# Group matmuls in four row tiles, a conditional residual layer on one Trainium2 core

## What is computed

```
masked_w = weight * mask[None, :, :]                 # (g, o, t)
w_bot    = einsum('bg,got->bot', y, masked_w)        # one 512 x 512 matrix for each batch
out      = x + einsum('bnt,bot->bno', x, w_bot) + bias
```

## Time and profile before

| | |
|---|---|
| median of 3 runs | 603.37 us |
| profiled execution, its own time | 604.59 us |
| its span, first to last instruction | 602.80 us |
| mean granted TensorE clock | 0.997 |
| TensorE matmuls, busy | 592.4 us (98%), 6343 records |
| VectorE busy | 320.9 us (53%) |
| ScalarE busy | 142.3 us (24%) |
| data moved | 148.33 MB, mean 246 GB/s |

### The profile page before, as it was taken

How to read it: one execution, slowest core, us unless ns; L and a number is a source line. 1 busy time by engine, 2 the same in 40 slices (tenths; PEclk the granted TensorE clock), 3 DMA queues, 4 the chain that set the end, 5 groups by cost and what they waited for, 6 DMA issues and landing times.

```text
span 602.8 us, 14826 instructions
## 1 busy us (share of the span) xinstructions
PE 592.4 (98%) x6343; PEld 515.1 (85%) x6343; DVE 320.9 (53%) x525; ACT 142.3 (24%) x278; POOL 36.3 (6%) x33
## 2 busy tenths in 40 slices
PE   7899999999999999999999999999999999999998
PEld 5799988888888888888888888888888888888886
DVE  4565445546546556465565565555554654654342
ACT  5343222222222222222222222222222222220000
POOL 3330000000000113231000000000000000000000
PEclk8999999999999999999999999999999999999999
DMA  8976557676776899998766776767767776778852
GB/s 324 406 280 197 199 176 228 235 236 223 230 247 207 295 333 336 352 318 284 247 214 227 251 212 240 233 228 227 241 229 228 237 235 229 225 232 258 296 160 87
DMA packets 60833, 148.33 MB, mean 246 GB/s; under 512 B 6736, under 2 KB 9552, under 8 KB 60768
## 3 DMA queue, kind: packets, MB, share of 16 engines
q1 hardware_dynamic: 40176, 113.00, 58.2%
q10 hardware_dynamic: 20592, 34.39, 15.1%
HBM read 113.81 MB, written 33.55 MB: 244 GB/s over the span
## 4 chain that ended last, share of the span: by engine, by line
PE 94%; DMA 4%; issue 1%; DVE 1%; SPq 0%; POOL 0%; DVEq 0%; POOLq 0%
PE ps L446 73%; PE ps L423 20%; DMA staged<-in_xn 3%; DMA xs<-in_mask 1%; PE ps L406 0%; DVE staged L356 0%; POOL wm L193 0%; SPq L214 0%; DVE wbot L328 0%; DVE wm L193 0%; SPq L229 0%; SPq L220 0%; DVE staged L361 0%; DVE staged L342 0%; DVEq L165 0%
## 5 line engine op out<-in xcount | busy, mean ns | idle before, releaser
L446 PE MATMUL ps<-wbot,xs 128*128 128x256 f32 (+1 forms) x2176 | 459.3, 370 | 1.8 <-DVE wbot L328 1.5
L446 PEld LDWEIGHTS ps<-wbot,xs 128*128 128x128 f32 x2176 | 389.7, 190 | 56.6 <-issue 3.6
L328 DVE COPY wbot<-ps 128x512 f32<-128x512 f32 (+2 forms) x271 | 163.8, 650 | 208.7 <-PE ps L446 181.0
L268 ACT ACTIVATE wbot<-ps 128x512 f32<-128x512 f32 (+2 forms) x277 | 141.1, 568 | 399.4 <-PE ps L423 198.0
L423 PEld LDWEIGHTS ps<-y_sb,wm 32*128 32x128 f32 x4096 | 124.1, 188 | 23.4 <-issue 21.1
L423 PE MATMUL ps<-y_sb,wm 32*128 32x128 f32 x4096 | 137.2, 279 | 3.8 <-DVE wm L193 1.6
L356 DVE TENSOR_TENSOR staged<-ps,staged 128x512 f32<-128x512 f32 x111 | 76.2, 687 | 39.3 <-PE ps L446 39.1
L342 DVE TENSOR_TENSOR staged<-staged,bias_sb 128x512 f32<-128x512 f32 x112 | 78.4, 700 | 11.6 <-DMA staged<-in_xn 11.3
L193 POOL TENSOR_TENSOR wm<-wm,mask_sb 128x512 f32<-128x512 f32 x16 | 20.4, 1298 | 215.5 <-DMA mask_sb<-in_mask 215.5
L356 DVE TENSOR_TENSOR staged<-ps,bias_sb 128x256 f32<-128x256 f32 (+1 forms) x24 | 12.2, 510 | 12.9 <-PE ps L446 10.8
L193 POOL TENSOR_TENSOR wm<-wm,xs 128x512 f32<-128x512 f32 x12 | 15.1, 1270 | 23.0 <-DMA xs<-in_mask 22.9
(11 more groups left out here) (2 smaller groups left out, 0.2 us busy)
## 6 DMA issues: line engine op xcount, KB each, us to landing
xs<-in_x SPq DMA_DIRECT2D x128, 512.0 KB, 3.9
out<-staged ACTq DMA_DIRECT2D x119, 256.0 KB, 4.8
staged<-in_xn SPq DMA_DIRECT2D x112, 256.0 KB, 4.3
wm<-in_w SPq DMA_DIRECT2D x12, 512.0 KB, 7.0
mask_sb<-in_mask SPq DMA_DIRECT2D x8, 512.0 KB, 6.5
out<-staged ACTq DMA_DIRECT2D x18, 128.0 KB, 4.0
wm<-in_w SPq DMA_DIRECT2D x8, 256.0 KB, 5.6
xs<-in_mask SPq DMA_DIRECT2D x4, 512.0 KB, 12.8
```

The costliest lines, as they stand in the source:

```text
L268: eng.activation(tile_place(b, j, first, end), tile_sums(b, j, first, end), ACT.Copy).then_inc(s_ev_a, 1)
L328: eng.tensor_copy(tile_place(b, j, first, end), tile_sums(b, j, first, end)).then_inc(s_ev_v, 1)
L446: ins = eng.matmul(bank[:, at_h:at_h + width], xs[:, n % XRING, h, k, :], at, start=(k == 0), stop=(k == KT - 1))
```

## The change

TensorE works on pairs of pieces, four batches. Each of the four batches has a PSUM bank of its own. A pair is made in four **turns**: in turn t, batch i uses row tile (i + t) mod 4, that is 32 of the 128 rows of its contraction, over the four chunks of t; after four turns each batch has been through all row tiles, and its bank holds the whole sum. From the second turn on, batch i waits for the semaphore `s_turn[i]`, which its own last matmul of the former turn raises. The array stays in four row tiles for bursts and groups alike.

Bursts stand between the turns: in a usual pair half of the first burst after turn 0, its other half after turn 1, the second burst after turn 2 (`bursts_in`). Pairs and bursts use four banks each and swap them from pair to pair (`bank_of`, `USED`, `FORMER`): the bursts of a pair use the four banks of the pair before, one burst after the other in the same four, and the next pair takes them after that. The pair that opens a unit (`halved`, units 1 to 7) is made for its first 128 columns in four turns, with bursts after turns 1 and 2, and then for its other 128 in four more without bursts. Pairs 0 to 7 are the pieces of 128 columns; pair 4 has no burst. From piece 122 on, when all bursts are done, pieces are made as before on the whole array (`plain`); the last is made and stored in three parts (256, 128 and 128 columns).

VectorE's order in a pair: both additions of the pair before, the copies of the first burst, x+bias for the two pieces of the pair, the copies of the other bursts. A piece's sums are free to add once its whole pair is done (`done_at`). ScalarE: two stores, then the copies. SyncE loads x in twos; x for the addition goes ahead of them, and x step 7 ahead of the last w pair. SOON is 2, the mask of burst 7 goes to GpSimd, and tile 1 of burst 3 to VectorE.

```diff
+ENDING = ((0, 0, SL), (1, 0, SL // 2), (1, SL // 2, SL))
+PAIRS = (LAST + 1) // 2
+def bursts_in(p):
+    if p < EARLY // 2:
+        return {0: ((2, 8, 0, KT),),
+                1: ((0, 9, 0, 2), (1, 9, 2, KT), (2, 10, 0, KT)),
+                2: ((0, 11, 0, KT), (1, 12, 0, KT), (2, 13, 0, KT)),
+                3: ((0, 14, 0, KT), (2, 15, 0, KT))}[p]
+    b = 2 * p + 2 * CS - 26
+    if p == EARLY // 2 or b >= BURSTS:
+        return ()
+    if halved(p):
+        return ((1, b, 0, KT), (2, b + 1, 0, KT))
+    return ((0, b, 0, 2), (1, b, 2, KT), (2, b + 1, 0, KT))
+def halved(p):
+    u, g, _, _ = PIECES[2 * p]
+    return u > 0 and g == 0
+def done_at(m):
+    return TILES * (m // 2 + 1) if m < PLAIN else TILES * PLAIN // 2 + m - PLAIN + 1
...
+USED = [[], []]
+for _b in range(HALF):
+    USED[_b % 2].append(("burst", _b))
+for _p in range(PLAIN // 2):
+    USED[_p % 2].append(("pair", _p))
+    USED[1 - _p % 2] += [("burst", _b) for _b in bursts_of(_p)]
...
-BY_VECTOR = (0, 1, 3, 7)
+BY_VECTOR = (0, 1, 3)
...
+            for n in range(XRING, STEPS, 2):
+                m = DONE_WITH[divmod(n - XRING, GROUPS)]
+                if m + 4 >= OWN_X:
+                    load_xn(m + 4)
+                    load_xn(m + 5)
                 load_x(n)
+                load_x(n + 1)
+                if m // 2 in LOAD_W_AT:
+                    load_w(1, LOAD_W_AT[m // 2], 2)
...
+            for p in range(PLAIN // 2 + 1):
+                if p:
+                    add_sums(2 * p - 2)
+                    add_sums(2 * p - 1)
+                bursts = bursts_of(p)
+                for b in bursts[:1]:
                     evict(b)
+                for m in (2 * p, 2 * p + 1):
+                    if m >= OWN_X:
+                        add_bias_to_x(m)
+                for b in bursts[1:]:
+                    evict(b)
...
+            def turn(p, t, c, end, opening, closing, last):
+                u, g, first, _ = PIECES[2 * p]
+                cols = slice((c - first) * CO, (end - first) * CO)
+                for k in range(KT):
+                    for i in range(TILES):
+                        j = (i + t) % TILES
+                        rows = slice(j * TR, (j + 1) * TR)
+                        gi, h = g + i // GB, i % GB
+                        if opening and k == 0 and c == first:
+                            room(("pair", p), i)
+                        if not opening and k == 0:
+                            eng.wait_ge(s_turn[i], turns[0])
+                        at = sums[rows, gi, c:end, k, h, :] if u % 2 else sums[rows, c:end, gi, k, h, :]
+                        ins = eng.matmul(ps[:, p % 2 * TILES + i, cols], xs[rows, (u * GROUPS + gi) % XRING, h, k, :], at,
+                                         start=opening and k == 0, stop=closing and k == KT - 1)
+                        if k == KT - 1:
+                            ins.then_inc(s_s2 if last else s_turn[i], 1)
+                turns[0] += 0 if last else 1
+            def pair(p):
+                u, g, c, end = PIECES[2 * p]
+                first_end = HALF if halved(p) else end
+                group_ready(u, g, first_end)
+                group_ready(u, g + 1, first_end)
+                for t in range(TILES):
+                    turn(p, t, c, first_end, t == 0, t == TILES - 1, t == TILES - 1 and not halved(p))
+                    for at, b, step, to in IN_PAIR[p]:
+                        if at == t:
+                            burst(b, step, to)
+                if halved(p):
+                    group_ready(u, g, end)
+                    for i in range(TILES):
+                        turn(p, i + TILES - 1, first_end, end, i == 0, i == TILES - 1, i == TILES - 1)
```

More of the change, by code:

```diff
@@ L377, in _, with room, burst @@
         def _(eng):
[L378 to L389, removed]
+            def room(key, j):
+                former = FORMER[key]
+                if former is None:
+                    return
+                kind, at = former
+                if kind == "pair":
+                    eng.wait_ge(s_o, 2 * at + 2)
+                else:
+                    tile_evicted(eng, at, j, GROUPS)
+            def burst(b, step, end):
                 u, c = divmod(b, CS)
@@ L409, in add_x @@
                             ins.then_inc(s_s1, 1)
[L411 to L419, removed]
+                if step == 0:
+                    if b == 0:
+                        eng.wait_ge(s_y, 16)
+                    if b == CS:
+                        eng.wait_ge(s_y_rest, 16)
+                    if win == 0:
+                        masked(eng, s, c)
+                    if ahead:
+                        add_x()
@@ L420, in burst @@
+                for k in chunks[step:end]:
                     for j in range(TILES):
-                        if not ahead and k == others[0]:
-                            room((b, j))
-                        ins = eng.matmul(bank[j][:, k * P:(k + 1) * P], wm[rows[j], c, k * P:(k + 1) * P],
+                        if not ahead and k == chunks[0]:
+                            room(("burst", b), j)
+                        ins = eng.matmul(at(j, k), wm[rows[j], c, k * P:(k + 1) * P],
                                          y_sb[rows[j], win, :], start=not (ahead and k == own),
@@ L425, in burst, with group_ready @@
                                          stop=not (behind and k == own))
-                        if not behind and k == (others[-1] if ahead else own):
+                        if not behind and k == chunks[-1]:
                             ins.then_inc(s_s1, 1)
-                if behind:
+                if end == KT and behind:
                     add_x()
-            def piece(m):
-                u, g, c, end = PIECES[m]
+            def group_ready(u, g, end):
                 n = u * GROUPS + g
-                width = (end - c) * CO
@@ L435, in piece @@
                 eng.wait_ge(s_x[n % XRING], 16 * (n // XRING + 1))
                 if g in (0, SOON):
+                    b = u * CS + end - 1
+                    soon = g == 0 and len(parts_of(b)) > TILES
                     for j in range(TILES):
[L438 to L443, removed]
+                        tile_evicted(eng, b, j, SOON if soon else GROUPS)
@@ L452, in _ @@
             for _ in range(WARM):
-                eng.matmul(ps[BANKS - 1][:, :], zeros[:, 0:P], zeros[:, 0:BANK], start=True, stop=True)
+                eng.matmul(ps[:, BANKS - 1, :], zeros[:, 0:P], zeros[:, 0:BANK], start=True, stop=True)
             for b in range(HALF):
[L455 to L459, removed]
+                burst(b, 0, KT)
+            for p in range(PLAIN // 2):
+                pair(p)
+            for m in range(PLAIN, LAST + 1):
+                plain(m)
 LEAD = {_c: _c if _c < HALF else _c - _c % 2 for _c in range(CS)}
```

135 lines of the change are left out of this document (71 added, 64 removed).

## The result

The changed kernel took **635.7 us** (median of 4 runs, 630.7 to 650.5) against 603.2 before: 1.051 times as long, 95% interval 1.043 to 1.060. The forecast was 603.2, with a range up to 612. Slower was given 0.40, but not by so much.

What follows compares the result with a forecast made beforehand. TensorE, busy 98%, bounds the kernel. New work of 531.7 us against 531.2 gives +0.5; with -0.3 for mask 7 and -0.4 at the end, -0.2 us: median 603.2 us, no change, range 597 to 612.

Steps and rivals of the forecast that it cites:

- The round trip between the forms: Switching TensorE between bursts and groups costs 0.42 us; 61 such trips, 25.6 us, removed but half of the last.
- The wide slot in row tiles: 256-column slots in row tiles, taken as 0.216 us; rival: 2.7 ns more each, +4.0 us, 607.2; chance 0.12.
- Two copies in the shadow of a wide turn: Between a pair's bursts in the same banks: 1.78 us wait covered by a wide turn's 1.84, 0.06 to spare.
- A turn behind another: Turn directly after another waits for the same batch's former turn: 0.31 us lost, 34 uncovered turns, 10.5 us.
- An opening pair: Halved pair opening units 1 to 7: about 11.0 us against 9.2, its four uncovered turns included.
- Instructions: Rival: doubled TensorE instruction stream; one in five of 100 packets costing 1.25 us, +25, 628; chance 0.05.
- the cover of the additions: First burst of a wide pair waits for the former pair's additions: 1.93 us against 1.94, so nothing lost.
- To VectorE 0.11: Latency from a pair's last matmul record to VectorE's additions, 0.11 us within the 1.93 us wait.
- covers are too short: Rival: three waits in each of 46 wide pairs not covered; at 0.08 us longer latency +9.4, 612.6; chance 0.19.
- late VectorE: In the kernel before, 2.3 us lost between 209 and 253 us, VectorE late behind its loads; taken as removed.

Runs made afterwards that it cites:

- e6: Changed kernel's order, banks and loads, but each batch made on the whole array where its turn stood; 652.2 us, 1.080 of the kernel before.
- e2: Changed kernel without the loads of x transposed beyond the first ten steps, 62 MB less moved; 620.4 us, 1.027 of the kernel before.
- e1: Changed kernel run once more with no edit, for its trace and spread of times; 641.6 us, 1.059 of the kernel before.
- e12: Kernel before with its steady x and x+bias loads of two groups asked for together; 602.9 us, 0.9975 of the kernel before.
- e5: Changed kernel with the second x and x+bias load of each two held until the next pair's second turn is done; 622.9 us, 1.030 of the kernel before.
- the first trace: First profiled execution of the changed kernel, the longest of its four runs; 650.5 us.
- e4: Changed kernel with one semaphore increment and one wait a turn in place of four; 642.5 us, 1.060 of the kernel before.
- e7: Changed kernel with one increment in place of four at a pair's end only, turns keeping four; 643.6 us, 1.056 of the kernel before.
- e9: Kernel before with sixteen already satisfied waits (eight instructions) after each group matmul; 1137 us.

## Why the prediction was wrong

**What held.** The round trip between the forms costs 0.41 to 0.42 us and goes away (e6). The wide slot in row tiles is 0.216 us, so that rival is out. Two copies in the shadow of a wide turn fit. A turn behind another cost less than the 0.31 I took: its first matmul starts 0.33 us after the last slot began, where 0.11 is the pace, so 0.22, and its four waits come 0.04 us apart. An opening pair undisturbed takes 11.14 us for 11.05 (e2), which is partly luck: its four turns were 0.36 us cheaper than taken, so the rest was some 0.45 dearer.

**The step that failed** is the rival "Instructions", which the sum put at nothing. It was named, tied to the 1.25 us of "issue" in the earlier trace rows, priced at 25 us (one in five of 100 packets), and given 0.05, with the ground that "bursts issue at twice the new mean rate without a pause". A burst is 32 weight loads and 32 matmuls, 64 instructions in 0.9 us, after which groups issue 9 a microsecond; a short rush is no measure of what can be sustained. The mean went from 21 records a microsecond (12,894 of TensorE in 603 us) to 41 (26,367 in 637), and the instruction packets from 50 to 103:

```profile
q8 instruction: 103, 1.69, 1.1%
```

Stops came at 19 and 20 of the 103 blocks of 256, up to 3.3 us long, 17.6 to 25.5 us a run. The packets in the traces show what they are. In all 14 traces there is one packet of q8 (16 KB) for 256 records of TensorE: 103 for 26,367, 86 for 22,143, 60 for 15,342, 50 for 12,894. Of 1158 such blocks not one began less than 1.2 us after the end of its packet, and the 111 stops of over 0.31 us at the start of a block all ended 1.2 to 1.6 us after it; the one that ended at 278.22 us in e1 had its packet from 276.0 to 276.9. A packet lasts 0.95 to 0.98 us in the median of every run, so its own transfer is not what grows. What differs is when it starts, here counted from TensorE's entry into the block ahead of the one it brings (60 to 545 us of each trace):

| us | packet starts after: median, 90% within, longest | a block lasts: median, shortest |
|---|---|---|
| kernel before | 0.5, 3.6, 4.3 | 11.1, 6.6 |
| its loads in twos (e12) | 1.1, 4.5, 5.6 | 11.1, 6.6 |
| whole array (e6) | 0.8, 3.2, 4.8 | 12.7, 9.0 |
| changed kernel (e1) | 1.8, 3.9, 4.6 | 5.9, 4.2 |
| without x loads (e2) | 0.4, 1.3, 4.2 | 5.7, 4.2 |
| loads spread (e5) | 0.9, 2.8, 4.6 | 5.7, 4.2 |

The kernel before gets packets 4 us late too, and a block of 6.6 us or more hides it. In a block of 5.9 us, a packet that starts over some 3.7 us late (5.9 less 0.96 and 1.2, an estimate) stops TensorE. So it is the instructions per microsecond that failed. e6 alone would not show it, since it also lacks the turns' waits and has three round trips a pair. That data transfers have a part in how late a packet starts is shown by e2 and e5, and e12 has later packets than the kernel before without a stop. Why a packet starts late in one block and not in the next stays open.

**A second, smaller step**: what a stop does to the clock. The prediction counted no clock at all. 6.8 us in e1 went that way and some 9 in the first trace, which also has 7.9 us more of stops: together some 10 of the 12.0 us between these two executions. That the same makes the 3% spread of the others is likely, not shown.

**A third**: the cover of the additions, with 0.01 us to spare. "To VectorE 0.11" was the latency behind one matmul on the whole array. In e1 it is 0.24, in 37 of the 46 wide pairs. A pair's end there:

```profile
463.77 3.63 PE L519 MATMUL ps<-wbot,xs 32*128 32x256 f32 x64
...
465.92 1.29 DVE L401 TENSOR_TENSOR staged<-ps,staged 128x512 f32<-128x512 f32 x2 [0.61 <-PE ps L519]
...
467.26 0.73 PE L483 MATMUL ps<-y_sb,wm 32*128 32x128 f32 x16
...
467.81 1.91 PE L519 MATMUL ps<-wbot,xs 32*128 32x256 f32 x32
```

The pair's last slot starts at 463.77 + 7 x 0.216 = 465.28, and the last of its four records, which start within 0.02 us, ends at 465.68; VectorE starts at 465.92. The turn behind the half burst, due at 463.77 + 16 x 0.216 + 4 x 0.112 = 467.67, starts at 467.81. That is the 0.14 us of every wide pair, 6.4 us in all: the rival "covers are too short", priced at 9.4 for all its places, in this one place alone, since the two covers of the copies held. Three of the four increments make 0.08 of it: in e4 and e7 VectorE starts 0.16 us after the last record and the wide pair takes 8.75 us. The rule of the Trainium skill that spoke for the rival (TensorE: Matmul & The Clock Gate, The cost: per-tile semaphore tail) gives about 0.08 us for three further increments, an estimate. The trace agrees; I had set the rule aside for a row that showed only the first of four increments. The other 0.05 us, 0.16 for 0.11, have no cause that a run here shows.

**And what was right in part, for the wrong reason**: "late VectorE" of 2.3 us between 209 and 253 us was put down to loads. For the later of the two cases that holds (VectorE waited 1.40 us for a load before 250.25). In the earlier, the addition of x+bias at 219.19 took 1.74 us where 0.68 is usual, while GpSimd multiplied by the mask from 217.88 to 220.38. Only one of e1's 112 such additions was slowed (1.01 us), but in e2, where GpSimd's work falls at other times, seven that ran beside it took 1.66 to 1.76 us, and pairs 30, 31 and 34 there last 9.4 to 10.1 us, 2.7 us over 8.83 each in all. (Pair 32's 9.94 us holds a stop of 0.9.) So GpSimd's work beside VectorE is a cause as well as the loads; when the two meet was not tried.

Put right, the sum would have been 603 + 6 for the covers, + 16 to 24 for the stops beyond those of before, + 7 for the clock: 632 to 640.

## What to carry to other kernels

A change that keeps TensorE's work but doubles its instructions has to be costed by instructions a microsecond over several blocks of 256, and one "issue" stop in the old profile is a warning to be followed up: number the records, look whether the stops lie at equal distances, and look when the instruction packets end. Such stops depend on what the data queues do at that time, so loads asked for in bunches can cost TensorE time that no row puts down to a load. A cover with 0.01 us to spare is none: price it as a loss, once for each time that it stands in the loop.

## What the runs showed of the hardware

- TensorE's stops for instructions lie at fixed record numbers 256 apart, in the kernel before too (once, 1.4 us at 16.50 us), and their length changes from run to run (3.10 and 2.00 us at the same number).
- TensorE's stream came as one packet of 16 KB for 256 records in all 14 traces, and no block of 256 began less than 1.2 us after its packet's end. Packets started up to 4.3 us after TensorE entered the block before theirs in the kernel before, and up to 5.6 us when that kernel's loads were bunched.
- The same transfers, 1.5 MB or 0.75 MB asked for at a time, gave 17.6 or 9.5 us of such stops; at four times, in another kernel, they rose from 0 to 5.2 us.
- A stop of 1.7 to 2.2 us among narrow turns brought the clock from 2.4 to 1.2 GHz for 3.4 us, four times in one run; stops of 1.7 and 2.4 us in two traces did not.
- Additions of x+bias on VectorE took 1.66 to 1.76 us in place of 0.68 while GpSimd multiplied (e2, seven times).
- Waits for semaphores that had long been reached cost nothing at three instructions of two waits for each 0.43 us of whole-array matmuls, and 61 ns an instruction at eight (e9, clock 0.948).
- Four increments at the end of four row tiles' work held up the reader by 0.08 us against one.
